# Conditioned attention on one core: one projection product moved to the first slot of a step, and one load of x moved forward

## The reference

```
Q = split_heads(x @ Wq.T + bq);  K = split_heads(x @ Wk.T + bk);  V = split_heads(x @ Wv.T + bv)
cQ = Q + split_heads(cond @ Wq.T + bq)        # cond: one row per batch
cK = K + split_heads(cond @ Wk.T + bk)
scores = cQ @ cK^T / sqrt(32)
x + merge_heads(softmax(scores) @ V)
```

## Time and profile before

| what | value |
|---|---|
| median of 3 runs | 665.7 us (665.44 to 667.35) |
| profiled execution | 665.71 us, span 663.9 us |
| PE busy | 656.2 us, 99% of the span |
| DVE, POOL, ACT busy | 541.2, 485.5, 373.2 us (82%, 73%, 56%) |
| granted TensorE clock | 1.00 |

### The profile page before, as it was taken

One profiled execution on the slowest core, in us unless ns is written; L12 is line 12 of the kernel. 1 busy time (PEld: TensorE's weight loads), 2 busy tenths in 40 slices (PEclk: granted clock), 3 DMA queues, 4 the chain that ended last, 5 costly groups with the idle time before them and its releaser, 6 DMA issues.

```text
span 663.9 us, 10095 instructions
## 1 busy us (share of the span) xinstructions
PE 656.2 (99%) x3556; PEld 440.9 (66%) x3556; DVE 541.2 (82%) x819; ACT 373.2 (56%) x659; POOL 485.5 (73%) x202
## 2 busy tenths in 40 slices
PE   9999999999999999999999999999999999999997
PEld 6776776666676666676666676666676666675442
DVE  4686888888888888888888888888888888888887
ACT  6335665555655555655555655555655555555663
POOL 6518777779777779777779777779777778766890
PEclk9999999999999999999999999999999999999999
DMA  9844334554434554334554334554434544326401
GB/s 300 193 112 104 89 98 113 143 145 119 105 98 113 144 143 121 103 98 112 144 145 123 102 97 112 143 146 119 106 98 111 144 128 111 83 83 159 129 18 63
DMA packets 48278, 79.87 MB, mean 120 GB/s; under 512 B 9826, under 2 KB 9826, under 8 KB 48226
## 3 DMA queue, kind: packets, MB, share of 16 engines
q1 hardware_dynamic: 47700, 79.21, 44.3%
q10 hardware_dynamic: 528, 0.02, 0.0%
HBM read 19.95 MB, written 8.39 MB: 43 GB/s over the span
## 4 chain that ended last, share of the span: by engine, by line
PE 92%; DVE 4%; DMA 1%; SPq 1%; ACT 1%; issue 0%
PE bank L291 26%; PE bank L395 19%; PE bank L415 17%; PE bank L374 17%; PE bank L351 12%; DVE mf L700 3%; DMA xr<-xT 1%; PE bank L446 1%; DMA Pt<-xT 1%; SPq L947 0%; SPq L960 0%; PE bank L324 0%; PE bank L423 0%; ACT Pt L610 0%; PE bank L336 0%
## 5 line engine op out<-in xcount | busy, mean ns | idle before, releaser
L610 ACT ACTIVATE Pt<-bank 128x512 f32<-128x512 f32 x512 | 299.2, 600 | 224.4 <-PE bank L395 157.0
L700 DVE TENSOR_REDUCE mf<-bank 128x1 f32<-128x512 f32 x496 | 333.8, 685 | 78.6 <-PE bank L374 77.4
L887 POOL TENSOR_TENSOR A<-A,Pt 128x2048 f32<-128x2048 f32 x59 | 270.8, 4591 | 4.6
L395 PE MATMUL bank<-Qs,Ks 98*128 98x512 f32 x496 | 200.5, 407 | 1.3 <-ACT Pt L610 1.2
L374 PE MATMUL bank<-Ks,Qs 96*128 96x512 f32 x496 | 200.5, 404 | 0.3 <-DVE mf L700 0.3
L887 POOL TENSOR_TENSOR A<-Pt 128x2048 f32<-128x2048 f32 x30 | 138.0, 4599 | 2.8 <-DVE part_sums L725 2.0
L395 PEld LDWEIGHTS bank<-Qs,Ks 98*128 98x128 f32 x496 | 93.2, 188 | 60.2 <-ACT Pt L610 39.4
L857 POOL TENSOR_TENSOR Xl<-xr,Xh 128x512 fp32r<-128x512 f32 x28 | 36.0, 1288 | 117.8 <-ACT Xh L573 117.8
L415 PE MATMUL bank<-Pt,V 128*32 128x512 f32 x1024 | 119.1, 596 | 0.1
L374 PEld LDWEIGHTS bank<-Ks,Qs 96*128 96x128 f32 x496 | 93.7, 189 | 26.6 <-DVE mf L700 4.8
L291 PE MATMUL bank<-Xl,Wh 128*128 128x512 f32 x256 | 102.0, 398 | 0.2 <-DVE Xl L673 0.2
(11 more groups left out here) (70 smaller groups left out, 374.5 us busy)
## 6 DMA issues: line engine op xcount, KB each, us to landing
Qs<-hi SPq DMA_DIRECT2D x60, 256.0 KB, 3.6
Ks<-hi SPq DMA_DIRECT2D x60, 256.0 KB, 3.6
Qs<-lo SPq DMA_DIRECT2D x30, 256.0 KB, 4.1
Ks<-lo SPq DMA_DIRECT2D x30, 256.0 KB, 3.4
xr<-xT SPq DMA_DIRECT2D x28, 256.0 KB, 2.7
res<-xT SPq DMA_DIRECT2D x28, 256.0 KB, 2.9
outT<-ot SPq DMA_DIRECT2D x28, 256.0 KB, 3.2
Qs<-mt SPq DMA_DIRECT2D x124, 4.0 KB
```

The source lines that it names most:

```text
L395: e.matmul(st_bank(u)[:, :], k[0:98, j, kc * P:(kc + 1) * P], q[0:98, j, :], start=True, stop=True).then_inc(t_st, 1)
L610: e.activation(exponentials(g)[:, kc, j, :], st_bank(u)[:, :], ACT.Exp, scale=SCALE).then_inc(a_e, 1)
L700: e.reduce_max(to[:, 4 * j + qc:4 * j + qc + 1], MXB[u % 2][:, :], AXX).then_inc(v_mx, 1)
L887: e.tensor_tensor(sums, ex[:, 0, :, :] if kc == 1 else sums, ex[:, kc, :, :], ALU.add).then_inc(p_a, 1)
```

## The change

In steps 1 to 27 slot 0 holds one product instead of none and slot 11 two instead of three; the first slot of the list goes from 0 to 1, and the second keeps its one. Every product from slot 1 to slot 11 so stands one place earlier in the row of 36. SP loads chunk 3 of batch 1 right behind chunk 2, ahead of `maxima_rows(0)`, and no longer in its step 0; the later loads keep their places.

```
-PROJ = (0, 1, 3, 3, 3, 3, 3, 3, 3, 3, 3, 3, 2, 1, 1, 1)
+PROJ = (1, 1, 3, 3, 3, 3, 3, 3, 3, 3, 3, 2, 2, 1, 1, 1)
...
             load_x(1, 2)
+            load_x(1, 3)
             maxima_rows(0)
             stack(0, 2)
             stack(1, 2)
 
             for t in range(G - 3):
                 b, kc = divmod(t + 3, KC)
-                if b + 1 < B:
+                if b + 1 < B and t >= 1:
                     load_x(b + 1, kc)
```

## The result

The changed kernel took 661.47 us (median of 6 runs, 660.74 to 662.58) against 665.66 us of the kernel before in the same comparison: ratio 0.9932, 95% interval 0.9915 to 0.9948. Run again later beside more runs of the kernel before, it took 660.90 against 666.36: 0.9922 (0.9906 to 0.9938). So it is 0.7 to 0.8% faster, 4.2 us in the one comparison and 5.5 in the other. The forecast was 5.3 us, to 660.4, and the range 659.6 to 663.7 holds both medians.

A forecast was written before the change was run, and what follows sets the result against it. PE was taken to bound the kernel, busy nearly throughout with short waits hidden inside. Wait A 3.1, Wait B 1.2 and the load 1.0 sum to 5.3 us: 665.7 - 5.3 = 660.4 us, range 659.6 to 663.7.

The forecast's parts named there:

- Waits under a busy PE: In each step: PE is busy throughout, yet short waits hide there, seen as start distances above one pitch of 0.234 us.
- Wait A: Slot 1's maxima matmul waits for DVE's reduction of slot 15's: 0.12 us in each of 26 steps, 3.1 us won.
- Wait B: Slot 7's scores matmul waits for ACT's exponential of slot 5, behind V's copy: 0.046 us, 27 times, 1.2 us won.
- Slot 11, zero: Taking one product from slot 11 brings no new wait; slot 14's maxima matmul is clear by only 0.02 us.
- the return of the wait at M(14): Rival, chance 0.08: slot 14's maxima matmul waits since q's low part sits in slot 11; all 3.1 back, 663.5 us.
- a late load costs its full 0.19: Rival, chance 0.07: slot 14's maxima matmul begins only when its weight load ends; 1.6 us come back, 662.0 us.
- The load, 1.0 us: Step 0: moving x's chunk (1,3) earlier ends ACT's idle wait that delays slot 8's scores matmul, 1.0 us won.
- hidden anyway: Rival, chance 0.06: x's old load in step 0 already landed before ACT needed it; moving it brings nothing, 661.4 us.
- The upper bound of 1.3: Most the moved load could win in step 0, if K's stacking lands sooner without the load beside it: 1.3 us.
- Only the load counts: Rival, chance 0.04: the waits in slots 1 and 7 both turn into other waits, 664.7 us.
- Slower by late rows: Rival, chance 0.03: maxima's rows reach slot 0's scores matmul too late; 1 us late in 27 steps would give 672.

## Why the prediction was right

*Waits under a busy PE.* Right. PE's busy share is 99% in both profiles, and 3.8 us went out of 25 steps.

*Wait A, 3.1 us.* Right in mechanism and size: alone it was worth 3.0 us in time and 0.113 a step (26 x 0.113 = 2.9). The chain of 1.29 us against five or six pitches is confirmed from both sides: one matmul more between M(15) and M(1) removes the wait from slot 0 as well as from slot 15, and a product in slot 1, behind M(1), doesn't.

*Wait B, 1.2 us.* Right in mechanism: alone it was worth 1.15 us in time, with an interval of 0.5 to 1.6. By the chain it is smaller, 0.032 a step where 0.046 was read (27 x 0.032 = 0.9).

*Slot 11, zero.* Right, and with the narrow clearance that was named. Of the rivals, the return of the wait at M(14) is refuted for this list and shown to be real for one product fewer. The rival that a late load costs its full 0.19 falls too: in the changed kernel M(14) starts 0.14 after its load, before that load ends. The Trainium skill, "TensorE: Matmul & The Clock Gate", section "Architectural detail: the array is 16× 32×32, not 1× 128×128", says that a matmul can begin before its weights are all loaded; the trace agrees, with 0.14 here and 0.11 in the earlier trace rows, where the load came later. By these numbers a load may start an estimated 0.12 late (0.234 less 0.11) and cost nothing; 0.10 is the most that a run shows.

*The load, 1.0 us.* Right in mechanism; the size spreads, and the spread is M(7)'s. ACT's wait for x, 1.87 to 2.43 us in the profiles with the old load, is gone in all with the new one, so "hidden anyway" is refuted. With it falls the estimate by the fit of the Trainium skill's page "DMA: Bandwidth & Descriptors", which is one for each DMA on the GpSimd path. Here the old load stood behind six stacking transfers and took 5.17 us. In the new place, behind other transfers too, it took 5.6 us (27.4 to about 33), and the next one, at 57.4, 2.5. So the load did not get faster, it only began early enough; that the transfers ahead of it make it slow fits these numbers, but no run shows it alone. What PE gets is the 1.0 plus what M(7) lost before (0.14) less what it loses after, since M(7) waits for the stacked K, which the change leaves alone: 0.81 in the changed kernel's first profile (M(7) loses 0.34), 0.74 in its second (0.40), 1.14 with the load alone (nothing). In the kernel with two products in slot 1 and the old load M(7) lost as much as 0.78, so its wait differs without the load too; why it does is open. The upper bound of 1.3 stood on the stacking landing sooner, which is not seen: its last transfer took 5.2 us before and 5.1 and 5.5 after. In time the load alone brought 1.4 us, 0.8 to 2.0 by its interval, which holds the forecast.

*The total.* 5.3 forecast, 4.2 and 5.5 measured, intervals of 3.5 to 5.7 and 4.1 to 6.3. By the trace the steps gave about 4.0 us of the 4.3 (26 x 0.153) and the load 0.74 to 0.81 of the 1.0, so 4.7 to 4.8 in these executions, a little under the forecast. The profiled execution of the first comparison also began its scores 1.20 us late, which the change has no part in, and its 662.08 lies 1.18 above the 660.90 of the repeat. "Only the load counts" falls with the list alone, which won 3.9 us.

*Slower by late rows.* Refuted for this change. Its point of turning over was placed somewhat early: 0.77 us forecast from a spare of 0.57, about 1.0 by the spare of 0.8 that was measured; a delay of 1.17 us made the kernel 1.2% slower than before.

## What to carry to other kernels

Where an engine is "busy" all the time, read the distance between starts: one waiting matmul in a step of 109 was worth 0.12 us, and 26 of them half a per cent. For each matmul that reuses a buffer, add up the chain that frees it (matmul to reduction, reduction, semaphore, load) and count how many other matmuls stand in between; moving one matmul to the place where the count is one short removes the wait, if the place that it is taken from has one to spare. Check that spare in the same way, as a single pitch decided between nothing and 0.2 us a step.

## What was not expected of the hardware

The start of an execution differs by more than 1 us with the same instructions: S(0)'s load in step 0 came at 43.24 and at 42.15 us in the two profiles of the changed kernel. Over the eleven profiles of all kernels it came between 42.04 and 44.07, and it always waited for the maxima's rows, behind a chain that begins with the first loads. Differences of 1 us between single executions say nothing here.

In the kernel with the turning in slot 10, a 1.64 us wait of PE in the end part cost more than its length. Table by stretches around it (the second column is the stretch's length, then PE busy):

```profile
626.00:628.20 2.20, 0.56 (x4) 0.15 (x2) 1.02 (x3) 0.60 (x1) 1.24 (x3) 1.00 0.99 232
628.20:631.30 3.10, 3.10 (x7) 2.45 (x8) 1.40 (x2) 0.77 (x2) 3.10 (x1) 0.50 0.03 5
631.70:635.00 3.30, 2.86 (x11) 1.53 (x9) 2.12 (x4) 2.95 (x7) 0.17 (x1) 1.00 0.84 302
```

```profile
628.20 0.77 PE L374 MATMUL bank<-Xl,Xh 96*128 96x512 f32 x1 [1.64 <-DMA Xl<-lo]
628.76 0.63 PE L351 MATMUL bank<-Wvl,Xh 128*128 128x512 f32 x1
629.19 0.63 PE L395 MATMUL bank<-Qs,Ks 98*128 98x512 f32 x1
```

The late rows held up SP, the last group's stacking behind them came late, PE had been busy for only 0.56 of 2.20 us, and the granted clock behind it was 0.50, that is 1.2 GHz, for some 3 us: starts 0.43 apart instead of 0.23. Of this kernel's four runs three have a mean clock of 0.997 and took 673.84 to 675.57 us, and one has 0.999 and took 672.34. The profiles of the two kernels of the comparison show no such stretch; their mean clock is 1.00.
